# Self-attention on one Trainium2 core: the loop over the first three head groups written out on all engines

## What is computed

```python
q = (x @ Wq.T + bq).reshape(b, l, h, hd).transpose(0, 2, 1, 3)
k = (x @ Wk.T + bk).reshape(b, l, h, hd).transpose(0, 2, 1, 3)
v = (x @ Wv.T + bv).reshape(b, l, h, hd).transpose(0, 2, 1, 3)
scores = jnp.einsum('bhqd,bhkd->bhqk', q, k) / math.sqrt(hd)
scores = jnp.where(causal, scores, -jnp.inf)
att = jax.nn.softmax(scores, axis=-1)
out = jnp.einsum('bhqk,bhkd->bhqd', att, v)
out = out.transpose(0, 2, 1, 3).reshape(b, l, d)
return out @ Wo.T + bo
```

## Time and profile before

| what | value |
|---|---|
| median of 3 runs | 1999.88 us (1998.8 to 2001.1) |
| the profiled execution's own time | 2000.4 us |
| its span, from first to last instruction | 1998.4 us |
| TensorE busy | 1753.3 us, 88% of the span |
| VectorE busy | 1447.0 us, 72% |
| ScalarE busy | 941.6 us, 47% |
| GpSimd busy | 712.9 us, 36% |
| packets of the DMA queues that carry instructions | 120 of 1.97 MB in all (queue 8), 52 of 0.43 MB in all (queue 14) |

### The profile page before, as it was taken

The page is one execution under the profiler, slowest core; times in us unless marked ns, Lnnn a source line. Parts: engine busy times, 40 slices in busy tenths (PEclk is TensorE's granted clock), DMA queues, the critical chain, the costliest instruction groups (busy, mean ns, idle before and its releaser), DMA issues. The chain is left out here.

```text
span 1998.4 us, 45116 instructions
## 1 busy us (share of the span) xinstructions
PE 1753.3 (88%) x15496; PEld 1005.3 (50%) x15497; DVE 1447.0 (72%) x2229; ACT 941.6 (47%) x1565; POOL 712.9 (36%) x745
## 2 busy tenths in 40 slices
PE   6999999899999999999999999974688999999910
PEld 4666676455555555545555555543244555455500
DVE  5777888898898888988889888876753333333347
ACT  4556556665464654645546455444222333333334
POOL 6732023232232332322323223214344554445432
PEclk9999999899999999999999999995888999999965
DMA  8520011112121121211312213122313455643369
GB/s 265 119 44 23 3 56 49 54 64 96 54 97 54 64 96 54 97 59 59 110 40 96 82 36 117 39 70 80 106 64 118 143 186 170 227 156 114 109 230 313
DMA packets 82540, 200.37 MB, mean 100 GB/s; under 512 B 8704, under 2 KB 28544, under 8 KB 80320
## 3 DMA queue, kind: packets, MB, share of 16 engines
q1 hardware_dynamic: 63456, 136.89, 20.2%
q0 software_dynamic: 18912, 61.09, 9.9%
HBM read 141.86 MB, written 56.10 MB: 99 GB/s over the span
## 5 line engine op out<-in xcount | busy, mean ns | idle before, releaser
L1067 POOL TENSOR_TENSOR xa_xs<-xa_xs,sn 128x512 f32<-128x512 f32 x160 | 236.2, 1478 | 261.8 <-ACT xa_xs L1106 261.6
L382 PE MATMUL bank<-xhl,front_h 128*128 128x512 f16 x704 | 269.7, 383 | 20.7 <-DVEq L68 13.6
L383 PE MATMUL bank<-xhl,front_h 128*128 128x512 f16 x704 | 269.3, 382 | 0.0
L384 PE MATMUL bank<-xhl,front_l 128*128 128x512 f16 x704 | 268.9, 382 | 0.0
L1071 POOL TENSOR_TENSOR xa_sc<-xa_sc,xa_rs 128x1024 f32<-128x1024 f32 x32 | 62.2, 1945 | 447.1 <-DVE xa_rs L1286 447.1
L382 PE MATMUL bank<-out_h,xa_oh 128*128 128x512 f16 x512 | 194.2, 379 | 15.2 <-DVE xa_ol L1182 15.2
L384 PE MATMUL bank<-out_h,xa_ol 128*128 128x512 f16 x512 | 194.0, 379 | 0.0
L383 PE MATMUL bank<-out_l,xa_oh 128*128 128x512 f16 x512 | 194.0, 379 | 0.0
L1957 DVE SCALAR_TENSOR_TENSOR mo_z<-bank,mo_sg 128x256 f32<-128x256 f32 x80 | 34.0, 424 | 180.5 <-ACT mo_sg L1929 174.5
L1202 DVE TENSOR_TENSOR xa_rr<-xa_x,xa_xs 128x512 f32<-128x512 f32 x160 | 146.8, 917 | 1.5 <-POOL xa_xs L1067 1.3
L1153 ACT ACTIVATE xa_sc<-xa_sc 128x512 f32<-128x512 f32 x64 | 40.2, 629 | 227.8 <-DVE xa_sc L1221 227.8
(11 more groups left out here) (308 smaller groups left out, 4950.5 us busy)
## 6 DMA issues: line engine op xcount, KB each, us to landing
xa_rawc<-in_ew SPq DMA_DIRECT2D x33, 768.0 KB, 5.0
moe_ring<-scratch_w SPq DMA_DIRECT2D x16, 1536.0 KB
co_rows<-scratch_y SPq DMA_DIRECT2D x20, 1024.0 KB, 7.9
scratch_w<-xa_chunk_h SPq DMA_DIRECT2D x32, 384.0 KB, 2.3
scratch_w<-xa_chunk_l SPq DMA_DIRECT2D x32, 384.0 KB, 3.1
raw_front<-in_xwq SPq DMA_DIRECT2D x9, 1024.0 KB, 7.2
raw_out<-in_xwo SPq DMA_DIRECT2D x9, 1024.0 KB, 5.0
out<-raw_front SPq DMA_DIRECT2D x17, 256.0 KB, 6.8
```

What stands on the lines that cost most here:

```text
L382: pe.matmul(out_ap, ah, bh, start=start and m == 0, stop=False)
L383: pe.matmul(out_ap, ah, bl, start=False, stop=False)
L384: mm = pe.matmul(out_ap, al, bh, start=False, stop=stop and m == n - 1)
L1067: PO.mark(pool.tensor_tensor(xr, xr, sn[:, :].rearrange("p (a s) -> p a s", a=1) .to_broadcast([P, QT // S, S]), ALU.mult), f"sm{r}", st)
```

## The change

The loops over the first three rounds become loops of the program that builds the kernel: the four steps of each round are written out, one round behind the other, on SyncE, ScalarE, VectorE and TensorE. The fourth round's text is as it was.

```diff
-                    with sp.Fori(0, NG - 1) as i:
+                    for i in range(NG - 1):
                         front_weights(i + 1)
                         sp.wait_ge(DV.sem, DV.value("wol", Step(i, 0)))
...
-                    with act.Fori(0, NG - 1) as i:
+                    for i in range(NG):
                         for q in range(NQ):
-                            step(i, q)
-                    for q in range(NQ):
-                        step(NG - 1, q, True)
+                            step(i, q, i == NG - 1)
...
-                    with dve.Fori(0, NG - 1) as i:
+                    for i in range(NG):
                         for q in range(NQ):
-                            step(i, q)
-                    for q in range(NQ):
-                        step(NG - 1, q, True)
+                            step(i, q, i == NG - 1)
...
-                    with pe.Fori(0, NG - 1) as i:
+                    for i in range(NG):
                         for q in range(NQ):
-                            step(i, q)
-                    for q in range(NQ):
-                        step(NG - 1, q, True)
+                            step(i, q, i == NG - 1)
```

## The result

The changed kernel takes 1985.22 us (median of 6 runs, 1981.32 to 1990.27) beside 2000.73 us for the kernel before (6 runs): a ratio of 0.9922, interval 0.9904 to 0.9940.

What follows compares the result with a forecast made beforehand. The prediction took TensorE to bound the self-attention. From the profiled 2000.4 us it took 9.4 for the edges and 1.0 for the start, giving 1990.0, or 1989.5 us for the median, range 1986 to 1995.

Steps and rivals of the forecast that it cites:

- The two taken branches: Self-attention, edges after rounds 1 and 2: TensorE's waits for the branch target's code and their aftermath go, 9.4 us gained.
- the lower of the two bounds: Self-attention edges: 7.4 us gained, from 5.75 of idle time and 1.7 of half clock, if the remaining 1.9 stays.
- only the idle time comes back: Self-attention edges: slow steps behind them are VectorE's and ScalarE's own backlog; gain 5.75 us, 1994.1 us; chance 0.12.
- The branches and register instructions of the other engines: Self-attention loop: branches of ScalarE, VectorE and SyncE cost nothing; register instructions ahead of waits 0 to 1.1 us, taken as 0.
- the engines getting back into step: Self-attention steps behind the two edges: the remaining 1.9 us of the 9.4, beyond idle time and half clock.
- The start: Self-attention steps 0 and 1: three holes of late code shrink; 1.0 us gained, bounds 0 and 8 us.
- Each hole shrinks by the work that is done ahead of it: Steps 0 and 1: fewer register instructions put the holes later in the work, shrinking them about 0.4, 0.4 and 0.6 us.
- Code that lies elsewhere: Everything behind the self-attention moves by 4808 instructions in TensorE's list; effect taken as 0.
- the rival on them: Cross-attention loop: seven branches idle up to 3.30 us each, kernel 2009 us; decides from 2.0 us idle each; chance 0.05.
- The start heals: Steps 0 and 1: all three holes and the half clock there go, 8 us gained, 1982.5 us; chance 0.07.

Runs made afterwards that it cites:

- run 1: The kernel before with only TensorE's loop written out, the other engines keeping theirs: 1988.91 us, ratio 0.9935.
- run 2: The kernel before with the loops of ScalarE, VectorE and SyncE written out, TensorE keeping its loop: 1998.82 us, ratio 0.9992.
- run 10: The changed kernel once more, timed and profiled again: 1984.15 us, ratio 0.9926.
- run 16: The kernel before with TensorE's loop alone written out, for a second profile: 1988.38 us.
- run 12: The kernel before, unchanged, for a second profile: 2000.43 us.
- run 14: The kernel before, unchanged, for a third profile: 1998.20 us.
- run 7: The changed kernel with TensorE's loop over the last seven cross-attention rounds written out too: 1985.71 us, ratio 0.9923.
- run 3: The changed kernel with 56 empty semaphore increments on TensorE ahead of the normalisation's loop in front of the router: 1992.76 us, ratio 0.9951.
- run 15: The changed kernel with 56 empty increments ahead of the normalisation's loop in front of the router, for a second profile: 1993.23 us.
- run 9: The kernel before with the loops of ScalarE, VectorE and TensorE over two rounds and the third written out: 1996.20 us, ratio 0.9982.
- run 13: The kernel before with 50 empty TensorE increments at the self-attention's start and 50 ahead of the normalisation before the router: 1997.94 us, ratio 0.9992.
- run 6: The kernel before with 50 empty semaphore increments at the start of TensorE's self-attention: 2002.89 us, ratio 1.0003.

## Why the prediction was right, and where it was wrong

**The two taken branches: the mechanism right, the size 6.6 us instead of 9.4.** The mechanism is shown by runs 1 and 2. All of the change makes steps 2 to 11 shorter by 8.3 us, but only 6.6 of them are TensorE's loop. That is below the lower of the two bounds, 7.4 and 9.4. It is what the idle times (5.7 us in the mean of three profiles) and the half clock (some 1.1 us, since it followed two holes of six) add up to. The term of 9.4 us was read from one execution of the kernel before, the slowest of its three profiles in these steps (189.1 us for steps 2 to 11; the mean is 188.4), and the changed kernel's own steps aren't all 17.97: step 11 has 18.30, and one profile of four (run 10) has a hole of 0.67 us in step 6 with half a clock behind it. The rival "only the idle time comes back" was half right. The echo outside the clock did belong to VectorE and ScalarE, but it came from their branches and register instructions, which the change removes too, and not from a backlog that stays.

**The branches and register instructions of the other engines: taken as nothing, they are 1.7 us.** The two parts of the sum that were set to 0 (the branches of ScalarE, VectorE and SyncE, and the register instructions with bounds of 0 and 1.1) can't be told apart by these runs. Most of the 1.9 us that I had booked as "the engines getting back into step" after TensorE's holes belongs here (runs 1, 2 and 16). So the term for the edges was too large and this one too small, and that the two together came out at 8.3, near 9.4, is in part luck.

**The start: 1.0 us forecast, nothing measured.** Steps 0 and 1 take 45.4 us together in the changed kernel's first profile and 45.1 in the kernel before's; the means are 44.8 and 45.0. The third hole is missing, but it is missing in runs 12 and 14 of the kernel before as well, so that this isn't the change's doing. The first two moved later in the work (the second shrank from 1.5 to 1.1 us in the mean, the first hardly), but the time at half clock behind them took back what the holes lost. That they are late code, as the prediction read them, fits the packets: each of the three starts again 1.3 to 1.5 us after one has landed. "Each hole shrinks by the work that is done ahead of it" left out that the clock behind a hole costs as much as the hole.

**"Code that lies elsewhere: I take 0": the step that failed.** I looked for the effect of the shift at the branches of the cross-attention, and found rightly that there is little (idle times of at most 0.6 us, and all together worth 2 us in run 7). They are six and not seven, so that the rival on them would have cost 6 × 2.79 = 16.7 us. I should have looked for every "issue" row behind the self-attention. The kernel before had one of 3.20 us among the router's gate products. Its place in the list moved by 200 instructions relative to the 256-instruction borders, and it went: 3.0 us (12.1 to 9.05 us, means of three and four profiles). This is shown from both sides, by runs 3 and 15, which bring it back, and runs 9 and 13, which lose it otherwise. The lengths and places in all eighteen profiles fit one account: the next block comes late where the block before it is filled with short matmuls. That the missing block is what TensorE waits for is read from the hole's place, which follows the counted border, and from the packet that lands 1.2 to 1.5 us before each restart; no row names the wait. From the first border's matmul to the restart 6.5 to 7.1 us pass in the seven profiles with a full hole, and the 128 matmuls of a block run in 3.5 us. At these rows the trace goes against a sentence of the Trainium skill, "Runtime: NRT & Kernel Launch", section "Instruction fetch mechanics", by which the crossing from one block to the next is mostly hidden. In a run of matmuls of 0.03 us each it isn't: 2.8 to 3.4 us stand open.

**The account.** Mean spans are 1997.7 before (3 profiles) and 1983.3 after (4), a difference of 14.4: 8.3 from the self-attention's steps, 3.0 from the router's hole, 0.15 from the start, 1.7 from how often the clock's short form was met (4.0 × (3/4 − 1/3)), and 1.2 that I can't place, about the scatter of a mean of so few. The forecast had 10.4. With the router's hole in it, it would have been 1986.5 us, 1.3 us from the measured median.

**The rivals.** The slower one, the cross-attention's branches, did not happen: the longest idle time before its keys in the changed kernel's first profile is this:

```profile
1192.14 0.39 PE L382 MATMUL bank<-ch,front_h 128*128 128x512 f16 x1 [0.49 <-DVE xa_sc L1215]
```

In the other three profiles it is at most 0.55 us. The point from which it would decide was 2.0 us. "The start heals" forecast a time (1982.5) that is near the measured one, for a reason that was wrong: both large holes of the start are still there, 2.16 and 1.45 us.

**A better version.** None of the sixteen beats the changed kernel by more than the scatter. Writing the cross-attention's loop out as well costs instructions and gives nothing that can be measured.

## What to carry to other kernels

A taken branch on TensorE back over a body that is loaded anew each round cost 1.9 to 3.4 us of idle time in these kernels, and now and then a stretch at half clock behind it (two of six times in the kernel before, some 1.6 us each). Written out, the same body had no hole at these places, so that here it was worth writing out a loop of few rounds on the engine that bounds, and on that engine first. Such an edit shifts all later code of the engine: look through the whole trace for "issue" idle time among short matmuls, before and after, since those holes come and go with the code's place and may be as large as the effect that is sought. When two versions differ in code size, compare several profiles of each by stretches that have the same instructions, and distrust a releaser that had long been done.

## What the runs showed of the hardware that was not expected

- A hole among short matmuls follows the place of the code in the engine's list: 2.8 to 3.4 us with two borders of 256 instructions inside 192 gate products (7 profiles), and with one border 1.18 us (run 7), about 0.3 us (run 13) or none (9 profiles). It stands 3 to 5 matmuls behind a border and ends 1.2 to 1.5 us after a packet of the instruction queue has landed. The holes among matmuls of 34 columns at 70.33 us in run 6 (2.60 us) and at 258.36 in run 9 (1.45 us) end in the same way, 1.4 us after a packet.
- The half clock behind a hole isn't fixed by its length or place: it followed the first edge's hole in one profile of the kernel before, the shorter second one in another, and neither in the third.
- A short hole can cost more by the clock than by itself: 1.45 us of idle time and then 6.83 us at a granted clock of 0.50, 4.1 us in all.
- The clock behind the router is granted in two ways, 21.5 or 24.4 us for the same 106 matmuls, in executions of one and the same kernel.
- An increment of a semaphore on TensorE isn't free: 200 of them took at most 32.34 us, 0.16 us each, while 56 were covered by a wait of 14 us.
